# Half the hidden features of the second edge layer as three rounded matmul pieces, with their low part made on VectorE and the first layer's activation moved ahead of the messages

## What is computed

```
h   = relu(layernorm(x))                                  # nodes, 256 features
e   = relu(raw @ W_e1.T + b_e1) @ W_e2.T + b_e2            # edges, raw has 64 features
emb = (e * (clip(polarity, 0, 1) + 0.01)) @ W_le.T + b_le
msg = relu(h[src] + emb)
agg = segment_sum(msg, dst)
out = x + relu(layernorm((h + agg) @ W_g1.T + b_g1) * ln_g + ln_b) @ W_g2.T + b_g2
```

## Time and profile before

| | us |
|---|---|
| three runs | 2511.22, 2511.51, 2516.98 (median 2511.51) |
| profiled execution, its own time | 2513.17 |
| its span, first to last instruction | 2511.5 |
| PE busy | 2341.1 (93%) |
| DVE busy | 1904.1 (76%) |
| ACT busy | 1586.8 (63%) |
| POOL busy | 1644.0 (65%) |

### The profile page before, as it was taken

One profiled execution on the slowest core, in us unless ns is written; L12 is line 12 of the kernel. 1 busy time (PEld: TensorE's weight loads), 2 busy tenths in 40 slices (PEclk: granted clock), 3 DMA queues, 4 the chain that ended last, 5 costly groups with the idle time before them and its releaser, 6 DMA issues.

```text
span 2511.5 us, 34919 instructions
## 1 busy us (share of the span) xinstructions
PE 2341.1 (93%) x10492; PEld 1946.3 (77%) x10492; DVE 1904.1 (76%) x3747; ACT 1586.8 (63%) x3112; POOL 1644.0 (65%) x1679
## 2 busy tenths in 40 slices
PE   5798999999999999999999999999999999999998
PEld 4677787877887787778877787877787787787876
DVE  7677777877787777777777777777787777777776
ACT  7566666666666666666666666666666666666664
POOL 6666666666666666666666666666666666666663
PEclk9899999999999999999999999999999999999999
DMA  9444444444444444444444444444444444444442
GB/s 311 131 132 129 132 146 131 139 130 134 145 140 136 131 145 139 135 133 141 139 136 133 133 135 143 134 137 132 137 143 137 134 134 143 137 137 134 141 140 60
DMA packets 136344, 349.07 MB, mean 139 GB/s; under 512 B 32019, under 2 KB 58325, under 8 KB 136149
## 3 DMA queue, kind: packets, MB, share of 16 engines
q0 software_dynamic: 77376, 211.39, 29.6%
q1 hardware_dynamic: 58772, 135.37, 15.8%
HBM read 333.82 MB, written 12.82 MB: 138 GB/s over the span
## 4 chain that ended last, share of the span: by engine, by line
PE 50%; DVE 27%; another core or an unknown queue 9%; issue 9%; ACT 4%; POOL 1%; DVEq 0%; DMA 0%; ACTq 0%; SPq 0%
PE bank L828 29%; DVE bank L676 11%; PE bank L844 9%; DVE mhl L686 7%; PE bank L806 5%; DVE oh L665 4%; PE bank L807 4%; DVE rlo L427 3%; ACT mhl L601 1%; PE bank L875 1%; PE bank L861 1%; ACT rhi L422 1%; POOL x_sba L371 1%; ACT hh L589 1%
## 5 line engine op out<-in xcount | busy, mean ns | idle before, releaser
L578 POOL DMA_INDIRECT hx<-gather_table,sidx x1612 | 1604.9, 996 | 823.7 <-issue 400.6
L828 PE MATMUL bank<-wc,hh 128*128 128x256 f32 x6448 | 1467.2, 380 | 2.7 <-issue 2.5
L828 PEld LDWEIGHTS bank<-wc,hh 128*128 128x128 f32 x6448 | 1218.9, 191 | 179.8 <-issue 9.2
L601 ACT ACTIVATE mhl<-bank 128x512 fp32r<-128x512 f32 x806 | 482.3, 599 | 842.1 <-DVE bank L676 671.7
L676 DVE SCALAR_TENSOR_TENSOR bank<-bank,gt,hx 128x256 f32<-128x256 f32 x1612 | 683.0, 484 | 380.1 <-remote 311.1
L686 DVE SCALAR_TENSOR_TENSOR mhl<-bank,mhl 128x512 fp32r<-128x512 f32 x806 | 549.7, 689 | 26.8 <-ACT mhl L601 1.8
L806 PE MATMUL bank<-rhi,w1r 128*128 128x512 f32 x806 | 379.8, 471 | 129.2 <-ACT hh L589 81.7
L589 ACT ACTIVATE hh<-bank 128x512 f32<-128x512 f32 x806 | 441.2, 601 | 28.2 <-remote 19.4
L594 ACT COPY bank<-c 128x512 f32<-128x512 f32 x802 | 450.5, 609 | 0.0
L844 PE MATMUL bank<-mhl,oh 128*128 128x512 f32 x1612 | 444.0, 397 | 0.5 <-DVE mhl L686 0.5
L665 DVE TENSOR_TENSOR oh<-iota,slot 128x512 fp32r<-128x512 f32 x403 | 279.2, 693 | 138.6 <-PE bank L844 80.7
(11 more groups left out here) (93 smaller groups left out, 479.7 us busy)
## 6 DMA issues: line engine op xcount, KB each, us to landing
raw<-in_attr_m SPq DMA_DIRECT2D x202, 512.0 KB
hx<-gather_table,sidx POOLq DMA_INDIRECT x1612
x_sba<-in_x SPq DMA_DIRECT2D x12, 512.0 KB, 8.9
gather_table<-x_sba SPq DMA_DIRECT2D x12, 512.0 KB, 7.7
xt<-in_x SPq DMA_DIRECT2D x48, 128.0 KB
out<-xt SPq DMA_DIRECT2D x48, 128.0 KB
dst_i<-in_dst_m SPq DMA_DIRECT2D x1, 805.5 KB
sidx<-in_src_m SPq DMA_DIRECT2D x1, 805.5 KB
```

Of the source, the lines that this page charges most:

```text
L578: eng.indirect_dma_start(out=hx[:, u % NX, j, :], out_offset=None, in_=tables, in_offset=bass.IndirectOffsetOnAxis(ap=sidx[:, t:t + 1], ax ...
L601: eng.activation(mh[:, u % 2, 2 * q:2 * q + 2, :], LB[(2 * u + q) % 4][:, :].rearrange("p (j n) -> p j n", j=2), ACT.Relu).then_inc(r_mh, 1)
L828: last = eng.matmul(o, hh[:, u % 2, k, e0:e0 + P], wc[:, k, :], start=False, stop=(j == 1 and k == 1), skip_group_check=seeded)
```

## The change

wc's first half gets a rounded copy and its rest (wcr, made by DVE before the loop). hh of the first half is now rounded to fp32r by ACT (hh), and DVE makes its rest (hl, new function `hidden_low`, one operation of 128x512); the second half stays float32 (hf). A tile of the second layer takes three fp32r matmuls of 256 columns (hh with wcr high, hh with wcr low, hl with wcr high) and one float32 matmul. `hidden_low(u+2)` stands between the two additions of unit u. On ACT the activation of the first layer runs two units ahead (it was one) and in front of messages; the rounding of raw features and the seeds stand behind them.

```diff
+        wcr = sb("wcr", [P, 2, D], F32R)
...
-                link(eng, eng.tensor_copy(c2r[0:1, :], c2[0:1, :]))
-                eng.tensor_tensor(c2r[32:33, :], c2[0:1, :], c2r[0:1, :].bitcast(F32),
+                eng.tensor_copy(c2r[0:1, :], c2[0:1, :])
+                link(eng, eng.tensor_copy(wcr[:, 0, :], wc[:, 0, :]))
+                eng.tensor_tensor(c2r[32:33, :], c2[0:1, :], c2r[0:1, :].bitcast(F32), ALU.subtract)
+                eng.tensor_tensor(wcr[:, 1, :], wc[:, 0, :], wcr[:, 0, :].bitcast(F32),
                                   ALU.subtract).then_inc(s_wt, 1)
...
-                        for k in range(2):
-                            eng.wait_ge(r_l1, 2 * u + k + 1)
-                            eng.activation(hh[:, u % 2, k, :], LA[k][:, :], ACT.Relu).then_inc(r_hh, 1)
+                        eng.wait_ge(r_l1, 2 * u + 1)
+                        eng.activation(hh[:, u % 2, :], LA[0][:, :], ACT.Relu).then_inc(r_hh, 1)
+                        eng.wait_ge(r_l1, 2 * u + 2)
+                        eng.activation(hf[:, u % 2, :], LA[1][:, :], ACT.Relu).then_inc(r_hf, 1)
...
-                        if u + 3 < UNITS:
-                            raw_high(eng, u + 3)
-                        if u + 1 < UNITS:
-                            hidden_high(u + 1)
+                        if u + 2 < UNITS:
+                            hidden_high(u + 2)
...
-                        if 1 <= u < UNITS - 1:
-                            seed(u + 1)
                         message_high(u, 0)
                         message_high(u, 1)
+                        if u + 4 < UNITS:
+                            raw_high(eng, u + 4)
+                        if u + 2 < UNITS:
+                            seed(u + 2)
...
+                    def hidden_low(u):
+                        if u >= 2:
+                            eng.wait_ge(r_l2, 2 * (u - 2) + 2)
+                        eng.wait_ge(r_hh, u + 1)
+                        eng.scalar_tensor_tensor(out=hl[:, u % 2, :], in0=LA[0][:, :], scalar=0.0,
+                                                 in1=hh[:, u % 2, :].bitcast(F32),
+                                                 op0=ALU.max, op1=ALU.subtract).then_inc(r_hl, 1)
...
                         total(u, 0)
+                        if u + 2 < UNITS:
+                            hidden_low(u + 2)
...
-                                eng.wait_ge(r_hh, 2 * (u - 1) + k + 1)
+                                eng.wait_ge(r_hf if k else r_hl, u)
...
-                        eng.wait_ge(r_hh, 2 * u + 2)
+                        eng.wait_ge(r_hl, u + 1)
+                        eng.wait_ge(r_hf, u + 1)
...
-                                for k in range(2):
-                                    last = eng.matmul(o, hh[:, u % 2, k, e0:e0 + P], wc[:, k, :],
-                                                      start=False, stop=(j == 1 and k == 1), skip_group_check=seeded)
+                                eng.matmul(o, hh[:, u % 2, e0:e0 + P], wcr[:, 0, :], start=False, stop=False,
+                                           skip_group_check=seeded)
+                                eng.matmul(o, hh[:, u % 2, e0:e0 + P], wcr[:, 1, :], start=False, stop=False,
+                                           skip_group_check=seeded)
+                                eng.matmul(o, hl[:, u % 2, e0:e0 + P], wcr[:, 0, :], start=False, stop=False,
+                                           skip_group_check=seeded)
+                                last = eng.matmul(o, hf[:, u % 2, e0:e0 + P], wc[:, 1, :],
+                                                  start=False, stop=(j == 1), skip_group_check=seeded)
```

More of the change, by code:

```diff
@@ L472, in edge_path @@
                     b = nodes(c, "a", s_o1, s_oa, 0, cx)
-                hh = sb("hh", [P, 2, 2, 512], F32, c)
+                hh = sb("hh", [P, 2, 512], F32R, c)
+                hl = sb("hl", [P, 2, 512], F32R, c)
+                hf = sb("hf", [P, 2, 512], F32, c)
                 oh = sb("oh", [P, 3, 4, P], F32R, c)
@@ L482, in edge_path @@
                 r_hh = sem("r_hh", c)
+                r_hf = sem("r_hf", c)
+                r_hl = sem("r_hl", c)
                 r_l2 = sem("r_l2", c)
@@ L634, in _ @@
                     raw_high(eng, 2)
+                    raw_high(eng, 3)
+                    hidden_high(1)
                     eng.wait_ge(s_wt, 2)
                     for u in range(UNITS):
-                        if u + 3 < UNITS:
-                            raw_high(eng, u + 3)
-                        if u + 1 < UNITS:
-                            hidden_high(u + 1)
+                        if u + 2 < UNITS:
+                            hidden_high(u + 2)
                         t = TILE_AFTER.get(u // GU - 1)
@@ L748, in _ @@
                     raw_low(eng, 2)
+                    hidden_low(0)
+                    hidden_low(1)
                     eng.wait_ge(s_sl, 1)
```

## The result

The changed kernel took 2595.97 us (2590.79 to 2598.25, 4 runs) against 2512.87 us (2511.22 to 2516.98, 4 runs) for the kernel before: a ratio of 1.0325, 95% interval 1.0304 to 1.0346. The forecast was 2507 us and its range ended at 2545; it was wrong. The profiled execution took 2590.79 us, its span is 2589.1 us.

The account below looks back on a forecast made before the run. The gathers' beat of 1.50 us, not TensorE, was taken to bound the loop. About 4.3 us returned in the loop and 1 us at the end gave a 2506.5 us span, forecast 2507 us, range 2420 to 2545.

Parts of the forecast that it names:

- ScalarE ... Cost 0: ScalarE's reordered work: same count and durations, no transfer moves, no DMA added, so 0 us.
- the seed moves behind them, with nearly a unit in hand: On ScalarE, the seed behind the relus and messages still has nearly a unit before second_layer(u+2) needs it.
- the beat of 1.50 us as a floor: POOL's gathers come at 1.50 us each, 2418 of the loop's 2422.3 us, and set the loop; chance 0.57.
- If POOL's pauses vanish, my reading of the beat was wrong: Sign on POOL: if its pauses between gathers vanish, the reading that the gathers' beat sets the loop fails, whatever the time.
- TensorE's term: Second layer: twelve pieces at 0.12 us replace eight float32 records at 0.216 us, -0.29 us a unit, -116 us of PE work.
- near 2225: Sign on TensorE: PE busy time falls to near 2341 - 116 = 2225 us, its idle time rising by as much.
- rival C: TensorE: short pieces' weight loads not hidden, 0.108 us twice a piece, +218 us, 2729 us; chance 0.03.
- VectorE's term: hidden_low on VectorE takes 0.69 us a unit, 278 us, paid from waits for gathers; DVE busy near 2182 us.
- floor of 5.59 us a unit: VectorE: 5.27 us of work plus 0.32 us unavoidable idle time a unit, 0.42 us under the gathers' beat.
- wait for the relu: VectorE's hidden_low waiting for ScalarE's relu: covered in the stretch examined, 0 to 0.7 us where DVE follows PE closely.
- B: VectorE becomes the bound through hidden_low's relu wait between additions: +72 us, 2583 us; sign DVE over 90% busy; chance 0.14.
- A: TensorE was the bound after all; VectorE's floor comes next: 85 us less, 2427 us, or 2342 without friction; chance 0.22.

Follow-up runs that it names:

- after_again: The changed kernel, unaltered, run again in a set where the kernel before hardly waits for gathers: 2465.81 us, ratio 1.0558 to the kernel before.
- a_dve_late: Changed kernel with VectorE's window_join and invert moved one stretch later, TensorE's turn left in place: 2302.91 us, ratio 0.986 to the kernel before.
- b_new_act_order: Kernel before with only ScalarE's new order (relus two units ahead, before messages; raw rounding and seeds behind): 2574.39 us, ratio 1.0234.
- pieces_old_order_2: Changed kernel with ScalarE's old order, hidden_low(u+1) behind onehot(u+1): 2267.22 us, ratio 0.9713; the same kernel earlier, with late gathers, 2612.96 us, ratio 1.0243.
- b_no_gate: Kernel before without the gathers' wait for the second layer three units earlier: 2597.37 us, ratio 1.034 to the kernel before.
- b_node_late: Kernel before with turn (TensorE), window_join and invert (VectorE) all moved later: 2334.7 us, ratio 0.9992 to the kernel before.
- p_no_gathers: Changed kernel with ScalarE's old order, without hidden_low, gathers for the first four units only: 2212.64 us, ratio 0.9468 to the kernel before.
- a_seed_front: Changed kernel with ScalarE's seed alone moved ahead, seed(u+1) opening unit u, relus still before messages: 2294.9 us, ratio 0.9826 to the kernel before.
- a_no_low: Changed kernel without VectorE's hidden_low; the third piece multiplies hh again: 2603.89 us, ratio 1.0353 to the kernel before.
- a_node_first: Changed kernel with ScalarE's window_out and root moved directly behind the messages: 2618.3 us, ratio 1.041 to the kernel before.

## Why the prediction was wrong, point by point

**What failed: "ScalarE ... Cost 0", and in it "the seed moves behind them, with nearly a unit in hand".** That sentence looked only at who needs the seed, the second layer of u+2. The forecast did note that the seeds hang on message_low. It did not ask what is queued behind the seed on ScalarE (window_out once a group, root in most), nor who waits for those: VectorE, at the operations directly behind message_low, the very one for which the seed waits. So once or twice in seven units DVE stood 1.4 to 1.5 us. Forecast 0; measured 149.8 us of waits, and 163 us returned when they go (after_again, a_dve_late), 171 with the seed moved back (across two sets). In sets with gathers in time this is shown. In a set with late gathers, the kind of the comparison that the forecast was for, ScalarE's order as a whole cost the kernel before 61 us (b_new_act_order) where the forecast said 0.

**What failed beside it: the beat of 1.50 us as a floor.** In the first comparison the stretches of 8 gathers went from 12.04 to a mean of 12.30 us, and 157 of them were counted where there had been 98. In the sets with gathers in time a_dve_late does a unit in 5.49 us and pieces_old_order_2 in 5.41, with the same 1612 gathers. Eight gathers are two units and twelve are three, so stretches of 12.0 and 18.0 us say that a unit takes 6.0 us, whatever sets that pace; they are no sign of a beat of the gathers' own. What sets the pace of late gathers no run shows: with their gate taken out (b_no_gate) a unit took 6.21 us. "If POOL's pauses vanish, my reading of the beat was wrong": they did not vanish (171 before, 223 after, 89 in b_node_late, 58 in a_dve_late, counted over 0.8 us), but they are no floor either, since the same kernel runs 7% faster on other occasions.

**TensorE's term was right** where TensorE is full: -0.30 us a unit against -0.29 (p_no_gathers), and the pieces come 0.12 us apart. Its sign in the changed kernel failed: PE was busy 2307 us, not near 2225. Some 46 of these 82 us are the lower clock; the rest no run takes apart. In a_seed_front, where the waits are gone, PE is busy 2189 us. The Trainium skill's rule that weight loads overlap only where row groups differ (TensorE: Matmul & The Clock Gate, Part 3, The mechanism) would have made rival C; the 2212.64 us of p_no_gathers speak against it here. The same section also names a background weight buffer as a second case of overlap, which the forecast passed over.

**VectorE's term was right in size**: hidden_low is 276.4 us of busy time against 278. DVE's busy time as a whole came to 2134 us, not 2182; the lengths of its instructions, added up, grew by 277 us, and they lie over one another more. Its floor of 5.59 us a unit was none: a_dve_late does a unit in 5.49 us and pieces_old_order_2 in 5.41, so the 0.32 us kept as unavoidable were not. Its wait for the relu measured 132.1 / 403 = 0.33 us a unit, inside the 0 to 0.7 given.

**The rivals.** B had the direction, and the time near (2583), with DVE first in the chain, but not the mechanism: DVE was 82% busy where B's sign said over 90, and a_no_low takes the wait inside the unit away and gains nothing. With gathers in time the waits that cost are behind message_low. A was right about the kernel before wherever gathers are in time, and pieces_old_order_2 shows its gain: 68 us against the 85 worked out. C fell.

**The clock** had no term. With gathers late, stretches at the lower level cost PE about 46 us more than before (each 20-us window's busy time, from 60 us on, times what its clock lacks of 1, summed: 61 against 15). With gathers in time it went with the waits: mean clock 0.983 in after_again and 0.994 in a_dve_late, and the same sum 30 and 5. So up to some 25 of the 163 us may be clock.

**What stays open.** In the sets with late gathers the two waits are just as long, but a_node_first, which removes them there, gained nothing; a_dve_late and a_seed_front did not run in such a set. There it is shown only that the order alone costs the kernel before 61 us where the changed kernel lost 83; what makes the other 22, and which of the order's waits makes the 61, stays open. Some of the loss is covered there: late gathers cost the kernel before 173 us (2512.87 against 2340.08 without) and the kernel after 131 (2595.97 against 2465.32), across sets. What makes gathers late, and what GpSimd's pauses are, no run settles.

## What to carry to other kernels

When an operation is moved back on an engine that works in order, ask first what is queued behind it and who waits for that, and only then who needs the operation itself. A short step that runs once in seven units can cost more than its busy time says: list the idle time ahead of the small groups, not only that of the large ones. And before a pace is called a floor, change the work beside it: stretches of equal length showed a pattern here, not a limit.

## What the runs showed that was not expected

- The kernel before took 2513 to 2550 us in three sets and 2336 to 2337 in three others, with runs within a set no more than 9 us apart. An experiment's ratio holds for its set alone: pieces_old_order was 1.0243 in one kind and 0.9713 in the other.
- Starting gathers earlier made the kernel before 3.4% slower (b_no_gate).
- A pause of TensorE of 2.3 us was often followed by 3 to 4 us at half the clock, but not always. From 60 us on, TensorE stood still for over 2 us 46 times in the kernel after, and 23 of the 38 stretches at half clock that began there came within 7 us behind such a pause; in after_again it was 46 times, and 16 of 19.
